# Eight PSUM banks in attention: two for row maxima in place of three, two for small jobs in place of one

## What is computed

```python
x = _layernorm(x + _L0_attn_ref(x, Wqkv, Wproj))          # causal attention, 16 heads of 8, projection
x = _layernorm(x + _L0_ffn_ref(x, ...))                   # mixture of experts
x = _layernorm(x + _L1_attn_ref(x, Wq, Wk, Wv))           # attention without mask, no projection
x = _layernorm(x + _L1_ffn_ref(x, ...))                   # dense network
# attention: rotary embedding of q and k, softmax(q k^T * 8**-0.5) v
```

## Time and profile before

| | us |
|---|---|
| three runs, median | 1450.9 |
| lowest, highest | 1447.1, 1459.64 |
| the profiled execution | 1459.25 |
| its span, first to last instruction | 1457.5 |
| busy: TensorE, VectorE, ScalarE, GpSimd | 1224.3, 923.8, 791.2, 520.8 |

### The profile page before, as it was taken

The page is one execution under the profiler, slowest core; times in us unless marked ns, Lnnn a source line. Parts: engine busy times, 40 slices in busy tenths (PEclk is TensorE's granted clock), DMA queues, the critical chain, the costliest instruction groups (busy, mean ns, idle before and its releaser), DMA issues. The chain is left out here.

```text
span 1457.5 us, 28689 instructions
## 1 busy us (share of the span) xinstructions
PE 1224.3 (84%) x10443; PEld 711.0 (49%) x10443; DVE 923.8 (63%) x2838; ACT 791.2 (54%) x1543; POOL 520.8 (36%) x476
## 2 busy tenths in 40 slices
PE   3399888888994976883499999999999959999996
PEld 1245444444443645761144344334343348888885
DVE  3367876678756592537488898888898251345443
ACT  1056655566564833433067677767677635555553
POOL 3225543555322674753303113113110014445452
PEclk9999999999896988995589999999999879999998
DMA  4502212321103103441712122132120000000000
GB/s 103 68 3 46 39 23 31 45 40 27 28 3 112 37 0 95 109 74 20 131 25 31 17 45 32 15 45 31 16 46 2 2 15 8 15 14 15 27 9 15
DMA packets 55948, 53.26 MB, mean 37 GB/s; under 512 B 8000, under 2 KB 38720, under 8 KB 55824
## 3 DMA queue, kind: packets, MB, share of 16 engines
q1 hardware_dynamic: 50528, 47.81, 17.1%
q0 software_dynamic: 3696, 2.76, 1.4%
q10 hardware_dynamic: 1600, 1.05, 0.3%
HBM read 15.74 MB, written 8.06 MB: 16 GB/s over the span
## 5 line engine op out<-in xcount | busy, mean ns | idle before, releaser
L427 ACT ACTIVATE a_prob<-a_ps_s 128x512 f32<-128x512 f32 (+1 forms) x896 | 466.5, 572 | 295.7 <-PE a_ps_s L508 272.5
L594 DVE TENSOR_REDUCE a_mx<-a_ps_m 128x1 f32<-128x512 f32 x512 | 329.2, 685 | 81.9 <-PE a_ps_m L523 80.0
L523 PE MATMUL a_ps_m<-a_kst,a_qst 24*128 24x512 f32 (+3 forms) x1024 | 278.4, 472 | 53.9 <-DMA a_qst<-a_lo_q 38.5
L591 DVE CUSTOM_DVE_ANT_0 a_junk<-a_ps_m,maskw 128x384 f32<-128x384 f32 (+3 forms) x512 | 227.3, 486 | 112.4 <-PE a_ps_m L523 112.0
L545 PE MATMUL a_ps_o<-a_prob,a_vst 128*32 128x256 f32 (+2 forms) x3840 | 279.5, 377 | 14.5 <-ACT a_oT L435 9.9
L508 PE MATMUL a_ps_s<-a_qst,a_kst 25*128 25x512 f32 (+3 forms) x1024 | 247.3, 457 | 22.7 <-ACT a_prob L427 13.7
L508 PEld LDWEIGHTS a_ps_s<-a_qst,a_kst 25*128 25x128 f32 x1024 | 108.9, 190 | 178.5 <-ACT a_prob L427 104.6
L459 PE MATMUL a_ps_s<-a_kst 128*32 128x256 f32 x2000 | 164.6, 403 | 3.6 <-ACT a_prob L427 3.5
L523 PEld LDWEIGHTS a_ps_m<-a_kst,a_qst 24*128 24x128 f32 x1024 | 124.4, 196 | 82.8 <-issue 53.3
L360 POOL TENSOR_SCALAR_AFFINE_SELECT a_prob<-a_prob 128x512 f32<-128x512 f32 x128 | 79.8, 635 | 228.7 <-ACT a_prob L427 228.7
L545 PEld LDWEIGHTS a_ps_o<-a_prob,a_vst 128*32 128x32 f32 x3840 | 85.1, 111 | 114.4 <-issue 62.6
(11 more groups left out here) (292 smaller groups left out, 1929.8 us busy)
## 6 DMA issues: line engine op xcount, KB each, us to landing
a_kst<-a_hi_k SPq DMA_DIRECT2D x128, 64.0 KB
a_qst<-a_hi_q SPq DMA_DIRECT2D x128, 64.0 KB
f_w<-in_L_ffn_W_dram SPq DMA_DIRECT2D x21, 256.0 KB
a_kst<-a_lo_k SPq DMA_DIRECT2D x64, 64.0 KB
a_qst<-a_lo_q SPq DMA_DIRECT2D x64, 64.0 KB
x_tiles<-in_L_attn_x_dram SPq DMA_DIRECT2D x8, 256.0 KB, 4.9
normed_rows_dram<-f_nrm SPq DMA_DIRECT2D x8, 256.0 KB, 2.3
f_hT_hi<-expert_sums_dram SPq DMA_DIRECT2D x4, 512.0 KB, 6.1
```

Of the source, the lines that this page charges most:

```text
L427: act.activation(prob[k][:, i, 0:w], ps_s[g % SB][:, 0:w], ACT.Exp, scale=float(D) ** -0.5)\
L523: last = pe.matmul(ps_m[g % MB][:, col:col + w], qst[r][lo_row:end, t, P * j:P * j + P], kst[r][lo_row:end, t, 0:w], start=True, stop=True)
L591: ins = dve.tensor_tensor_reduce(junk[g % MB][:, col:col + w], bank[:, col:col + w], maskw[:, T - w:T], 1.0, -3.0e38, ALU.add, ALU.max, out)
L594: ins = dve.reduce_max(out, bank[:, col:col + w], AX.X)
```

## The change

One line of `attention`: MB goes from 3 to 2 and XB from 1 to 2. All eight banks stay in use. `maxima`, `reduce_unit`, `ring` and the buffers `ps_m`, `junk` and `ps_x` (L267, L277, L279) take their number from it, in both calls.

```diff
@@ -239,7 +239,7 @@
     sh = Shapes(causal)
     U = sh.units
     G = B * NG
-    SB, MB, XB = 3, 3, 1
+    SB, MB, XB = 3, 2, 2
     START = [("xT", 0), ("k", 0), ("q", 0), ("v", 0), ("xT", 1), ("k", 1), ("q", 1), ("maxT", 0)]
     END = [("norm", G - 1)] + ([("yT", B - 1), ("proj", B - 1)] if causal else [])
     place = sh.ring(START, END, XB)
```

## The result

| | before | after |
|---|---|---|
| median, us | 1450.9 (four runs) | 1554.6 (four runs) |
| lowest, highest | 1447.1, 1459.64 | 1544.82, 1572.33 |
| profiled execution, its span | 1459.25, 1457.5 | 1544.82, 1543.1 |
| mean granted clock of TensorE | 0.917 | 0.891 |
| busy: TensorE, VectorE, ScalarE, GpSimd | 1224.3, 923.8, 791.2, 520.8 | 1302.2, 936.9, 794.2, 520.7 |

The change made the kernel slower: ratio 1.069, 95% interval 1.065 to 1.074. One run of the four after, 1572.33 us, is over 1.5% slower than the fastest and is left out of the ratio, but not of the median. The forecast was 1525, with a range of 1484 to 1556; the loss is 100 us by the ratio and 104 by the medians, where 74 were summed. The two profiled executions are 85.6 us apart.

The account below looks back on a forecast made before the run. TensorE and VectorE both had little room in the second stage, the causal stage being looser. Terms 56 + 5.4 + 2.5 + 11 - 1 = 74 us on the 1450.9 median gave 1525 us, range 1484 to 1556.

Parts of the forecast that it names:

- Maxima, second stage: Second stage's loop: odd maxima wait for the pair before's second reduction, 1.93 us a group over 29 groups, 56 us.
- Starts of the stages: Maxima issued before any score, with VectorE the bound: 5.4 us more in the second stage, 2.5 in the causal one.
- Small bank: Jobs wait for the job before last's reading: -1 us in the second stage, 1.9 a batch won in the causal stage.
- Stacked k and q: Causal stage, mid-batch: a 1.48 us wait for SyncE's stacked k and q absorbs 1.5 us of each batch's stalls.
- Causal loop: Causal stage: 4.9 us of maxima stalls less 1.9 and 1.5 leave 1.5 a batch, 11 us over 7.5 batches.
- The third rival: Second stage: stalls also lower TensorE's clock, 20 us on top, 1545, or 1565 with twice the share; 14%.
- Its test: A granted clock below 0.97 in the second stage's profile would mean the clock had fallen as well.
- The rule on banks and the clock: Skill's warning that short idle times between matmul groups make the clock oscillate; no row showed it for 0.4 us idle times.
- The sum's own range: Whole kernel: 1500 to 1545 us by the terms' bounds, with 67% for the forecast as summed.
- the small bank decides: Rival: reductions end early enough, only the small-job bank's gain of 11 us is left, 1440; 4%.
- the stalls are hidden: Rival: odd maxima wait only where ScalarE's exponentials already idle TensorE, 9 us left, about 1455; 4%.
- waits at L594 of some 80 us: Sign of being right: TensorE's waits of maxima for VectorE at L594 grow from 3.3 us to some 80.

Follow-up runs that it names:

- The stage alone: New banks (two for maxima, two small) in the second attention stage only, causal stage as in the kernel before: 1508.6 us, ratio 1.038.
- the filler: Four unread warm matmuls added after step 7 of each causal group: changed kernel 1521.3 us, ratio 1.047; kernel before 1444.8 us, ratio 0.994.
- filler and two small banks: Changed kernel plus four unread warm matmuls after step 7 of each causal group: 1521.3 us, ratio 1.047 against the kernel before.
- The whole causal stage: New banks in the causal stage only, second stage as in the kernel before: 1492.6 us, ratio 1.029.
- filler and one small bank: Changed kernel with one small bank, plus four unread warm matmuls after step 7 of each causal group: 1531.7 us, ratio 1.056 against the kernel before.
- the run without it: Two banks for maxima but one for small jobs, against the kernel before: 1559.4 us, ratio 1.076.
- the late order of maxima: Odd steps' maxima issued after values, warm matmuls and jobs: 1684.7 to 1790.5 us with two maxima banks, 1520.8 to 1778.4 with three; no ratio given.

## Why the prediction was right, and where it failed

- **Maxima, second stage (56 us): the mechanism right, the size too high.** The condition for the odd unit, the 0.05 us from a reduction to its matmul, and the alternation of stalls came out as worked out: 1.92 for 1.90, a group of 14.99 for 15.23. One step was off, the first, 1.29 for 1.51. Groups took 15.0, 14.7, 15.5 and 14.4 at full clock, where the sum had 15.2, 15.0, 16.2 and 15.2; the third and fourth were too dear, by 0.7 and 0.8. So the stalls cost about 41 us (59.66 - 53.95 = 5.71 a batch, 29/4 batches), and the loop's other 9 go with a clock of 0.947 in place of 0.958. The stage alone, 56.5 us by time, is near the 60 forecast, in part by luck: stalls priced 15 us too high, and a loss of clock that the sum didn't have.
- **Starts of the stages (5.4 and 2.5): right in the second, 4.6; too high in the causal one, 0.8.**
- **Small bank (-1, and 1.9 a batch in the causal term): counted twice.** The waits at L475 and L486 are gone, but in the causal stage they are gone with one small bank too, once the maxima have two: the stalls take their place, and the sum took them off beside the stalls. They were priced at 1 + 7.5 x 1.9 = 15 us, where the earlier trace rows has 10.1 for the causal stage. By the ratios the second small bank wins 10 us in the change, within the noise, and 13 beside the filler.
- **Stacked k and q (1.5 a batch): the wait of 187.78 is gone.** A later TensorE covers it. But 7.5 x 1.5 = 11 us were taken off, and the stage before had 5.2 us of such waits, in four places.
- **Causal loop (11 us): this is the term that failed.** The stalls were found and priced: with the clock at 0.995 on both sides two banks for maxima cost 21 us, where the sum without the small bank has 7.5 x (4.9 - 1.5) = 25, and with filler and two small banks 12 us is left, at the clock of before. But 4.9 us of stalls a batch were added to the timeline as time at an unchanged clock. In the kernel after, two stalls close together at units 8 and 9 stand ahead of each fall to 1.2 GHz, and the third of a batch's slowed groups is new. That loss of clock is 19 to 26 of the loop's 31 us. The batch that was read for the price was itself a slowed one. The whole causal stage cost 39.6 us by time.
- **The third rival, the clock, was the right mechanism in the wrong stage.** It was placed in the second stage, with 20 us; there the four groups read the earlier trace rows were at 1.00, and the whole loop went only from 0.958 to 0.947. The causal stage stood at 0.93, which should have been read as a stage in which idle times of this length already cost clock: two of its groups showed 0.87 and 0.89, and only the halves were looked at, not the groups. Its test was badly posed as well: 0.97 for the second stage, when the whole stage was at 0.958 before.
- **The rule on banks and the clock.** The Trainium skill, TensorE: Matmul & The Clock Gate, section "A second HAM failure mode: psum-queue depth-cycling", tells of short idle times between matmul groups cycling through PSUM banks that make the clock oscillate. The causal stage agrees: three falls a batch, behind idle times of 0.3 to 0.9 us. An idle time of that length doesn't always do it, as the seven batches with filler and one small bank show. The second stage doesn't show it in most groups, where the stalls fall between matmuls that keep TensorE busy for 14.37 of 14.99 us.
- **The range.** The sum's own range, 1500 to 1545, missed the 1554.6; the stated one, up to 1556, just held it, because it left room for a loss of clock in the other stage. That is in part luck.
- **Rivals of the other side.** That the small bank decides fell with the run without it; that the stalls are hidden fell with the group of 14.99 us.
- **The tests.** VectorE's busy time stayed within 1.5%, and the causal batch of 173.15 takes 51.07 us, just above the 49 to 51 named. The test "waits at L594 of some 80 us" failed as put and would have misled: TensorE's row has 19.4. It is the weight loads' row that shows 72.9.

What stays open: why the late order of maxima lets the clock stay low for hundreds of us, and why a wait of 0.91 us brings a fall in every batch with two small banks and in one of seven with one. That idle time at units 8 and 9 brings the falls rests on the filler's runs, which fill the first of two idle times, and on where the falls begin; how long one must be was not measured, since no run set the length of a stall by itself.

## What to carry to other kernels

Before a bank is moved, work out the cycle of each ring (matmul, reader's latency, the pair's reading, the next start) and compare it with the shortest steps, not the mean: with three banks the odd maxima waited for a reduction that let it start 1.30 us after the pair before, under steps of 1.43; with two it is 1.90, above them, and two banks for scores are too few as well. Price a new stall twice, once as time and once as what it does to the clock, and read the clock group by group in the kernel before: a stage with groups below 1.00 already pays for its idle times in clock. Read more than one batch, too: the one that was priced was slowed, and others were not. A few matmuls that nobody needs, issued where TensorE would idle, can be worth more than the bank.

## What the runs showed of the hardware

- Two idle times of 0.3 to 0.9 us, about 0.7 to 1.3 us apart, stood ahead of 3.4 us at 0.50; with 0.64 us of unneeded matmuls in the place of the first, two of the three falls in a batch didn't come (1554.6 to 1521.3 us). Where one idle time of 0.91 us was left, the clock fell behind that alone in seven batches of seven, and in one of seven with one small bank.
- A lower clock needs no idle time in the record to last: 100.00 us busy of 100.00 at 0.50, for 478 us, in the late order.
- A stall among matmuls that had run side by side shows as TensorE's busy time: 12.68 to 14.37 us in a group with nothing more to compute, and only 19.4 us of waits in the stage.
